# Latent cross attention on one core: layer norm folded into the weights and the exponent, keys projected from a transposed context with split f32r matmuls, batch end moved into the next round

## What is computed

```
def layernorm(x, g, b):
    mu = jnp.mean(x, axis=-1, keepdims=True)
    var = jnp.mean((x - mu) ** 2, axis=-1, keepdims=True)
    return (x - mu) * jax.lax.rsqrt(var + LN_EPS) * g + b
def rmsnorm(x, gamma):
    norm = jnp.sqrt(jnp.sum(x * x, axis=-1, keepdims=True)) * x.shape[-1] ** (-0.5)
    return x / jnp.maximum(norm, RMS_EPS) * gamma
xn = layernorm(x, ln_x_g, ln_x_b)          # x: context, (32, 1601, 192)
ln = layernorm(latents, ln_l_g, ln_l_b)    # (32, 64, 256)
q = ln @ Wq.T
kv = jnp.concatenate([xn @ Wkv.T, ln @ Wlkv.T], axis=1)
k, v = kv[..., :INNER], kv[..., INNER:]    # 4 heads of 64
attn = einsum('bhid,bhjd->bhij', rmsnorm(q, qn_g) * SCALE, rmsnorm(k, kn_g))
attn = softmax(where(full_mask, attn, -max))
out = einsum('bhij,bhjd->bhid', attn, v) @ Wo.T + bo
```

## Time and profile before

| | before |
|---|---|
| median of 3 runs | 4133.69 us (4133.42 to 4134.72) |
| the profiled execution | 4131.72 us |
| its span, first to last instruction | 4129.9 us |
| stage `xa_` | 166.9 to 1659.0 us of the span |
| mean granted TensorE clock | 0.873 of full speed |
| busy: TensorE, VectorE, ScalarE, GpSimd | 3298.8, 2627.2, 1901.4, 315.2 us |

### The profile page before, as it was taken

How to read it: one execution, slowest core, us unless ns; L and a number is a source line. 1 busy time by engine, 2 the same in 40 slices (tenths; PEclk the granted TensorE clock), 3 DMA queues, 4 the chain that set the end, 5 groups by cost and what they waited for, 6 DMA issues and landing times. The chain is left out here.

```text
span 4129.9 us, 98958 instructions
## 1 busy us (share of the span) xinstructions
PE 3298.8 (80%) x34538; PEld 2869.4 (69%) x34538; DVE 2627.2 (64%) x8299; ACT 1901.4 (46%) x3959; POOL 315.2 (8%) x323
## 2 busy tenths in 40 slices
PE   3489999999999999445437999999999999753664
PEld 3378888888888888333326888888888888633443
DVE  5477777777777775476666777777677777455000
ACT  1145555555555554123224666666566666422110
POOL 0200000000000000000012111111111111000101
PEclk7689998999999998677667999999999999965786
DMA  1111111111111110200011111111111111121322
GB/s 62 59 35 37 38 43 38 39 41 39 39 42 39 38 42 12 67 20 20 10 31 37 39 39 40 39 42 37 39 40 39 40 39 39 45 65 57 124 91 76
DMA packets 206334, 181.47 MB, mean 44 GB/s; under 512 B 65260, under 2 KB 199457, under 8 KB 205728
## 3 DMA queue, kind: packets, MB, share of 16 engines
q1 hardware_dynamic: 203808, 168.59, 14.2%
q0 software_dynamic: 2048, 6.68, 0.5%
HBM read 146.95 MB, written 28.39 MB: 42 GB/s over the span
## 5 line engine op out<-in xcount | busy, mean ns | idle before, releaser
L1768 DVE CUSTOM_DVE_ANT_0 xb_junk<-xb_ring,xb_mbias 128x372 bf16<-128x372 f32 (+2 forms) x1024 | 544.4, 572 | 175.7 <-PE xb_ring L1676 153.5
L1607 ACT ACTIVATE xb_P<-xb_sc 124x1024 f32<-124x1024 f32 (+1 forms) x416 | 426.0, 1026 | 377.0 <-PE xb_sc L1700 374.7
L704 PE MATMUL xa_ring<-xa_wf,xa_xT 96*124 96x256 f32 (+1 forms) x1664 | 399.8, 391 | 18.6 <-DVE xa_xT L818 15.3
L704 PEld LDWEIGHTS xa_ring<-xa_wf,xa_xT 96*124 96x124 f32 (+1 forms) x1664 | 313.9, 192 | 76.7 <-issue 23.7
L679 PE MATMUL xa_acc<-xa_xhat,xa_P 124*128 124x193 f32 x1664 | 314.1, 330 | 0.0
L1647 PE MATMUL xb_ring<-xb_xst,xb_whi 128*128 128x372 f32 (+2 forms) x768 | 262.2, 369 | 38.7 <-DVE xb_xst L1747 32.8
L1676 PE MATMUL xb_ring<-xb_khi,xb_qhi 64*128 64x372 f32 (+2 forms) x1024 | 266.1, 401 | 27.4 <-DVE xb_klo L1753 17.2
L1647 PE MATMUL xb_ring<-xb_whi,xb_xst 128*124 128x256 f32 (+1 forms) x1248 | 285.3, 291 | 2.4
L1700 PE MATMUL xb_sc<-xb_qhi,xb_khi 64*124 64x256 f32 (+1 forms) x1664 | 281.7, 372 | 0.0
L1753 DVE TENSOR_TENSOR xb_klo<-xb_ring,xb_khi 128x372 fp32r<-128x372 f32 (+2 forms) x256 | 138.6, 571 | 210.3 <-ACT xb_khi L1573 209.4
L679 PEld LDWEIGHTS xa_acc<-xa_xhat,xa_P 124*128 124x128 f32 x1664 | 267.2, 190 | 5.5 <-issue 5.5
(11 more groups left out here) (391 smaller groups left out, 7475.5 us busy)
## 6 DMA issues: line engine op xcount, KB each, us to landing
xa_raw<-in_ctx SPq DMA_DIRECT2D x64, 279.0 KB
ex_w<-in_W SPq DMA_DIRECT2D x16, 1024.0 KB
xa_raw<-in_ctx SPq DMA_DIRECT2D x32, 372.0 KB
xb_raw<-in_ctxT SPq DMA_DIRECT2D x64, 186.0 KB
xb_raw<-in_ctxT SPq DMA_DIRECT2D x32, 248.0 KB
xa_mask<-in_mask SPq DMA_DIRECT2D x32, 200.1 KB
xb_mask<-in_mask SPq DMA_DIRECT2D x32, 200.1 KB
xa_raw<-in_ctx SPq DMA_DIRECT2D x32, 186.0 KB
```

What stands on the lines that cost most here:

```text
L704: i = nc.tensor.matmul(bank[0:KEYS, 256 * (t % 2):256 * (t % 2) + 256], xT[0:H + h, c % 2, h, t * KEYS:(t + 1) * KEYS], wf[0:H + h, h, 0:256],
L1607: nc.scalar.activation(P[0:w, pbuf(c, p), :], sc[(c + p) % 2][0:w, :], ACT.Exp).then_inc(sem("exped"), 1)
L1768: v.tensor_tensor_reduce(out=junk[:, k, 0:w], in0=ring[f % 3][:, 0:w], in1=mbias[:, p, k0:k0 + w], scale=1.0, scalar=-3.0e38, op0=ALU.add, ...
```

## The change

The layer norm no longer produces xhat. The mean is folded into the weights: from each column of the gained weight matrix wf its mean over the 192 inputs is subtracted (with the matrix `even`). Keys are projected as x W + sigma b, which is the old key times sigma, and the RMS norm removes the factor. The values use raw x with a column sigma beside it, and P is divided by sigma in the exponent: the Exp has the bias nlr = -ln(var + eps)/2, one per key.

x comes already transposed from memory (input ctxT, which the stage `xb_` reads too). x and the weights are split in f32r parts, high and low, and the keys are the sum of five f32r matmuls for each tile. The parts that make x: ScalarE rounds 128 rows to xh (L712), GpSimd rounds the other 64 rows twice (L670, L671), VectorE subtracts to get the low parts (L952, L953). sigma is split too, on a tile `sig`, transposed by TensorE (step ST) and copied to rows of xhs by ScalarE (L707).

The new steps: Y (VectorE's statistics), YA (ScalarE: Ln, Exp, Copy, and nlr on GpSimd), YB (VectorE: low part of sigma), ST, X (splitting x), RS and R (the former R1 and R2), Q (GpSimd's preparation of a batch), PV (the weighing, now a step of its own). Y, YA, YB, ST, X and the first chunk of K run two batches ahead of B. F1 and F2 of a batch move into the next round, after the ring. M goes through the ring and is copied by one ScalarE instruction. The Exp is split in two of 256 columns. raw is three batches deep, STEADY is 12.

```
-        ROUNDS = [("T", 0), ("X1", 1), ("M", 0), ("K", 0), ("B", 0), ("X2", 1), ("X1", 2), ("R1", 0), ("T", 1),
-                  ("R2", 0), ("B", 1), ("K", 1), ("KT", 0), ("X2", 2), ("B", 2), ("X1", 3), ("R1", 1), ("A", 0),
-                  ("T", 2), ("R2", 1), ("B", 3), ("X2", 3), ("K", 2), ("KT", 1), ("X1n", 0), ("R1", 2), ("B", 4),
-                  ("A", 1), ("T", 3), ("R2", 2), ("B", 5), ("K", 3), ("X2n", 0), ("R1", 3), ("B", 6), ("KT", 2),
-                  ("PVend", 0), ("R2", 3), ("A", 2), ("KT", 3), ("F0", 0), ("F1", 0), ("A", 3), ("AL", 0),
-                  ("mred", 0), ("F2", 0)]
+        ROUNDS = [("Q", 0), ("K", 1), ("B", 0), ("R", 0), ("X", 3), ("RS", 1),
+                  ("B", 1), ("PV", 0), ("KT", 0), ("R", 1), ("K", 2), ("Yn", 0), ("RS", 2),
+                  ("B", 2), ("YAn", 0), ("PV", 1), ("A", 0), ("KT", 1), ("R", 2), ("YBn", 0), ("F1", 0),
+                  ("B", 3), ("PV", 2), ("A", 1), ("STn", 0), ("Xn", 0), ("K", 3), ("RS", 3), ("Yn", 1),
+                  ("B", 4), ("YAn", 1), ("PV", 3), ("KT", 2), ("R", 3), ("YBn", 1), ("F2", 0), ("Yn", 2),
+                  ("B", 5), ("YAn", 2), ("PV", 4), ("A", 2), ("STn", 1), ("Xn", 1), ("KT", 3), ("YBn", 2), ("Yn", 3),
+                  ("B", 6), ("YAn", 3), ("PV", 5), ("A", 3), ("AL", 0), ("STn", 2), ("Xn", 2), ("YBn", 3), ("mred", 0), ("STn", 3),
+                  ("Kn", 0), ("RSn", 0), ("PV", 6), ("M", 0), ("F0", 0)]
...
                 if kind == "K":
-                    pe.wait_ge(sem("xT0"), nth(n, 4, c))
-                    pe.wait_ge(sem("xT1"), nth(n, 4, c))
+                    pe.wait_ge(sem("xlo"), nth(n, 4, c))
+                    pe.wait_ge(sem("srow"), nth(n, 4, c))
...
+                            nc.tensor.matmul(o, xh[:, keys], wh[:], start=True, stop=False)
+                            nc.tensor.matmul(o, xh[:, keys], wl[:], start=False, stop=False)
+                            nc.tensor.matmul(o, xhl[:, keys], whh[:], start=False, stop=False)
+                            nc.tensor.matmul(o, xl[:, keys], wh[:], start=False, stop=False)
+                            i = nc.tensor.matmul(o, xhs[:, keys], wls[:], start=False, stop=True)
...
+                if kind == "ST":
+                    pe.wait_ge(sem("siglo"), nth(n, 4, c))
+                    bank = room((kind, c, 0), n)
+                    for t in range(nt):
+                        i = nc.tensor.transpose(bank[0:96, t * KEYS:(t + 1) * KEYS], sig[0:KEYS, t0 + t, :].bitcast(F32), ident[0:KEYS, 0:KEYS])
+                    i.then_inc(sem("st_ps"), 1)
...
+                if kind == "YB":
+                    dve.wait_ge(sem("sighi"), nth(n, 4, c))
+                    v.tensor_tensor(sig[0:KEYS, t0:t0 + nt, 65], raw[0:KEYS, t3, t0:t0 + nt, DC], sig[0:KEYS, t0:t0 + nt, 64].bitcast(F32),
+                                    ALU.subtract).then_inc(sem("siglo"), 1)
+                if kind == "X":
+                    dve.wait_ge(sem("xhi"), nth(n, 4, c))
+                    dve.wait_ge(sem("xhi2"), nth(n, 4, c))
+                    cols = slice(k0, k0 + W)
+                    v.tensor_tensor(xl[:, cols], xTr[:, 0, cols], xh[:, cols].bitcast(F32), ALU.subtract)
+                    v.tensor_tensor(xhl[64:128, cols], xTr[0:64, 1, cols], xhl[0:64, cols].bitcast(F32), ALU.subtract).then_inc(sem("xlo"), 1)
...
+                    nc.gpsimd.tensor_copy(xhl[0:64, k0:k0 + W], xTr[0:64, 1, k0:k0 + W])
+                    nc.gpsimd.tensor_copy(xhs[0:64, k0:k0 + W], xTr[0:64, 1, k0:k0 + W]).then_inc(sem("xhi2"), 1)
...
+                    nc.scalar.activation(P[0:KEYS, b_, 0:256], s_[0:KEYS, 0:256], ACT.Exp, bias=nlr[0:KEYS, t, 2 * c:2 * c + 1])
+                    if c < 6:
+                        i = nc.scalar.activation(P[0:KEYS, b_, 256:512], s_[0:KEYS, 256:512], ACT.Exp, bias=nlr[0:KEYS, t, 2 * c + 1:2 * c + 2])
```

More of the change, by code:

```diff
@@ L465, in schedule, with there, one @@
+        while len(FILLS) % len(ring):
+            FILLS.append(None)
+        PLACE = {f[0]: n for n, f in enumerate(FILLS) if f}
+        def there(n):
+            return not isinstance(n, int) or 0 <= n < NB
         def schedule(engine_step, loop_engine, chain=None, per_round=0):
-            def one(n, p, do_a, do_b, do_next):
+            def one(n, s):
                 for kind, c in ROUNDS:
                     if kind in OF_B:
[L470 to L480, removed]
+                        if there(n):
+                            engine_step(kind, c, n, s % 6)
+                    elif kind in OF_LAST:
+                        if there(n - 1):
+                            engine_step(kind, c, n - 1, (s + 5) % 6)
+                    elif kind in OF_NEXT:
+                        if there(n + 2):
+                            engine_step(OF_NEXT[kind], c, n + 2, (s + 2) % 6)
+                    elif there(n + 1):
+                        engine_step(kind, c, n + 1, (s + 1) % 6)
@@ L481, in schedule @@
+            for n in (-2, -1, 0):
+                one(n, n + 6)
+            turns = (NB - 5) // STEADY
+            with loop_engine.Fori(0, turns) as i:
                 if chain:
@@ L685, in step @@
-            def step(kind, c, n, p):
-                t0, nt = CHUNKS[c % 4]
-                W = nt * KEYS
-                if kind == "T":
-                    pe.wait_ge(sem("xhat"), nth(n, 4, c))
-                    for h in range(2):
-                        bank = room((kind, c, h), n)
-                        hi = H + h
-                        for t in range(nt):
-                            i = nc.tensor.transpose(bank[0:hi, t * KEYS:(t + 1) * KEYS],
-                                                    xhat[0:KEYS, p, t0 + t, H * h:H * h + hi], ident[0:KEYS, 0:KEYS])
-                        i.then_inc(sem("xT_ps"), 1)
+                r, k = n - FILLS[f][4], f - 4
@@ new lines, in room @@
+                while True:
+                    if k < 0:
+                        k, r = k + len(FILLS), r - 1
+                        if isinstance(r, int) and r < -2:
+                            break
+                    if FILLS[k] is not None:
+                        _, name, per, j, d = FILLS[k]
+                        if there(r + d):
+                            pe.wait_ge(sem(name), nth(r + d, per, j))
+                            break
+                    k -= 4
+                return ring[f % 4]
@@ L730, in step @@
                     pe.wait_ge(sem("negmax"), nth(n, 1, 0))
-                    if not (isinstance(n, int) and n == 0):
-                        pe.wait_ge(sem("accT"), n)
+                    bank = room((kind, c, 0), n)
                     for o in range(2):
-                        i = nc.tensor.matmul(sc[0][0:33, 128 * o:128 * o + 128], negmax[:, o, :], ident[:], start=True, stop=True)
+                        i = nc.tensor.transpose(bank[0:65, 128 * o:128 * o + 128], negmax[:, o, :], ident[:])
                     i.then_inc(sem("m_ps"), 1)
                 if kind == "B":
-                    s = sc[(c + 1) % 2]
+                    s_ = sc[(c + p) % 2]
                     if c == 0:
```

439 lines of the change are left out of this document (258 added, 181 removed).

## The result

The change makes the kernel slower: 4456.59 us (median of 4 runs, 4455.23 to 4458.94) against 4133.56 (4 runs, 4133.00 to 4134.72), a ratio of 1.078, 95% interval 1.0765 to 1.0797. The forecast was 3980, faster. The profiled execution after took 4456.78 us, its span is 4455.0, the mean clock 0.844.

The account below looks back on a forecast made before the run. TensorE was taken as the bound; the steady round falls from 44.5 to 39.5 us, and 150 + 7 + 9 - 14 = 152 us off 4131.7 gives 3980. Range 3865 to 4050 us.

Parts of the forecast that it names:

- the last round: Last round, with no next batch: 29.1 us becomes PV, B, F1 and F2 only, about 20, saving 9.
- the start: Before the first F0: memory clearing 8 us, weights' delay 14, shorter first round 8; net 14 later, bounds 5 and 30.
- a sign that the forecast is wrong: Forecast wrong if TensorE's largest wait isn't ST 3's, the clock reads near 1.00, or VectorE is busy over nine tenths.
- The step that failed: DMA term: context loaded twice, 40 GB/s become about 75, but loads are issued a round or more ahead, costing nothing.
- GpSimd's additions: Casts, second mask row and small operations add 6.8 us a round on GpSimd; contention with VectorE costs 0.3.
- the sum: Steady round: 44.5 - 3.6 - 1.4 - 0.2 - 2.2 - 0.4 + 2.0 + 0.5 + 0.3 = 39.5 us.
- VectorE's tight row: Behind K 0: 13 us of VectorE work before F1 can use A 0's bank; 0.5 us of waits a round.
- ST 3's wait for YB 3: End of a round: TensorE waits 2.0 us for VectorE, bounds 1.0 and 3.0, then half clock for about 6.8 us.
- the first rival: The wait comes but the clock holds, 3878 us, or ST 3 hardly waits, 3818 us; chance 0.26.
- K: Key projection on TensorE: 26 f32 matmuls, 11.26 us, become 65 in f32r, 7.64 us; gain 3.6 a round.
- F1's wait for latn: TensorE's wait before F1 goes because F1 comes a third of a round later; gain 2.2 us a round.
- The last rival: Slower than before: every added GpSimd operation holds VectorE for its own length, 6.8 us a round; 4175 us; chance 0.04.

Follow-up runs that it names:

- experiment 1: Changed kernel with step Q moved from the head of the round to behind X 3: 4231.9 us.
- experiment 5: Changed kernel with the small loads issued behind B 6's scores instead of behind PV 6, Q left at the head: 4167.0 us.
- experiment 2: Changed kernel with GpSimd's two casts of X writing 4 columns instead of 372 or 496 in the batch loop: 4444.3 us.
- experiment 11: kernel 8 with GpSimd's casts of X writing 4 columns instead of 372 or 496 in the batch loop: 4037.9 us.
- experiment 9: kernel 8 with the seven folded-weight loads issued behind the first three context loads: 4035.3 us, first F0 at 320.4.
- experiment 10: kernel 8 with batch 2's first context loads issued behind batch 1's transposed context: 4036.5 us, first F0 at 321.2.
- experiment 13: kernel 8 plus three ST steps later, weight loads early and batch 2's context behind batch 1's transposed context: 3975.1 us, 0.9617 of the kernel before.
- kernel 6: kernel 4 with F1 moved behind PV 2: 4052.8 us.
- kernel 8: kernel 4 with F1 moved behind PV 2 and the small loads issued behind B 6's scores: 4040.4 us.
- kernel 4: Changed kernel with Q moved behind X 3 and YB 3 ahead of X 2: 4118.1 us.

## Why the prediction was wrong

The difference to the forecast is 477 us of the span: 29 steady rounds at 54.75 in place of 39.5, 442; round 30, which was to be 7 us shorter, 36.5 in place of 32.5, 4; the last round as forecast; the start 29; the rest of the program 1.

Of the 15.3 us that a steady round is too long, TensorE is idle for 11.9 and busy for 3.4. The clock can account for the 3.4: it is at half for 17 us of a round in place of 6.8, which by estimate costs up to 5 us. That the largest wait of TensorE was another than ST 3's was named beforehand as a sign that the forecast is wrong.

- **The step that failed** is in the part on GpSimd and DMA: "The loads are issued a round or more ahead. Nothing." It holds for raw and xT. It doesn't for the four small loads, which SyncE issues behind PV 6 and for which Q waits at the head of the very next round, with X 3's casts behind it on GpSimd. I had GpSimd's additions as lengths (6.8 us, near enough: 8.5 in all, 9 forecast) and as contention (0.3), and never asked what each of them stands behind in its queue. Experiments 1 and 5, two different ways to take the wait away, give 225 and 290 us back.
- **What is left behind that step**: the kernel of experiment 5 is still 187 us above the forecast. Its steady round is 44.8 us, 5.3 too long, and its waits are 7.9 us a round where the sum had 2.8: ST 3.7, F1 for a bank 2.1, KT for khat 1.2 and for the maxima 0.9. The sum had one wait of ST and 0.5 for A 0's bank, and nothing for KT.
- **The evidence was at hand.** That GpSimd waits through each round for small loads could be read in the trace before; it cost nothing there, as nothing urgent stood behind. The change put the casts of X in the same queue, and those of X 3 directly behind it.
- **VectorE's tight row** behind K 0 was seen, with X 3 in it, and priced at 0.5 us of waits, on the ground that TensorE comes as late. That reckoned with VectorE's work only; with the row held for 7.5 us by another engine KT 1 stands still.
- **ST 3's wait for YB 3**: forecast 2.0, measured 2.7 on average. Right in mechanism and place, and within its bounds. The fall of the clock came with it in 21 of 29 rounds, mostly for 3.4 us in place of 6.8; in the other eight the clock held, as the first rival had it. The longest slow stretch came with the wait I hadn't seen, 10 to 14 us.
- **K**: starts 0.12 us apart, as in the earlier trace rows. TensorE's busy time fell by 1.9 us a round, though 17 us of the round ran at half clock. F1's wait for latn is gone; the one for A 0's bank, forecast at 0.5, is 1.9.
- **The last rival**, GpSimd's operations holding VectorE for their full length, had the right sign and the right pair of engines, at 4175, and the wrong mechanism. The Trainium skill, page "SBUF — State Buffer", section "Who interferes with whom", warns of such contention. Where the two meet the trace agrees. After, in the start of the stage, a subtraction without and one with GpSimd's mask row beside it:
```profile
228.65 0.55 DVE L952 TENSOR_TENSOR xa_xl<-xa_xTr,xa_xh 128x372 fp32r<-128x372 f32 x1 [1.88 <-ACT xa_xh L712]
...
233.03 1.72 DVE L952 TENSOR_TENSOR xa_xl<-xa_xTr,xa_xh 128x372 fp32r<-128x372 f32 x1 [1.88 <-ACT xa_xh L712]
```
```profile
232.82 1.53 POOL L648 TENSOR_SCALAR xa_mbias<-xa_mask 128x1612 bf16<-128x1612 uint8 x1
```
0.55 us became 1.72. But in the loop they hardly meet, and experiments 2 and 11 price the length of the casts, some 2.7 us a round, at 12 and 3 us.
- **The start** was forecast 14 us late, bounds 5 and 30, and was 43. Clearing memory held the first load by 9.7 us (182.50 against 172.78), 8 forecast. The weights' delay was named; the second delay, batch 2's context in SyncE's queue in front of batch 1's transposed context, was not, and by experiments 9, 10 and 13 it had to go too before either gave anything. With both gone the first F0 is at 298.3.
- **The range** failed with them: it took in bounds of the known terms and no case in which a moved step stands behind a wait on an engine that the sum called hidden.

## What to carry to other kernels

An engine that executes in order is hidden only as long as nothing that others need stands behind its longest wait: before work is given to an idle engine, read what that engine idles for and where in its order, not only for how long. When a step is added, follow it through each queue that it passes: what is ahead of it, which of those waits for a DMA, and when that DMA is issued. A delay that proves to be worth nothing when it alone is taken away may have a second one behind it, so take both away before it is dropped.

## What was new about the hardware

- The length of one wait didn't settle what the clock did. Before, it fell in every round, at F1's wait of 2.2 us or within some 2 us behind it. After, of 18 waits of ST 3 of 2.4 to 2.5 us it fell in ten and stayed at 1.00 in eight; at the 11 longer ones, up to 3.2 us, it fell each time. At KT 1's waits of some 7 us it fell each time, between 0.8 and 4.6 us into the wait. Waits that are nearly all between 0.4 and 2.0 us, several in a round, left it at 1.00 in 26 of 29 rounds of kernel 6 and in 15 of 29 of kernel 8. What decides it is open.
- GpSimd's mask row of 1612 columns is slowed by VectorE as well: 1.53 us in after, and here, in kernel 4, 2.32 us beside VectorE's multiplication for khat (up to 2.34 in its 32 executions there):
```profile
936.96 0.96 DVE L966 TENSOR_TENSOR xa_khat<-xa_ksb,xa_krn 124x768 f32<-124x768 f32 x1
```
```profile
936.99 2.32 POOL L648 TENSOR_SCALAR xa_mbias<-xa_mask 128x1612 bf16<-128x1612 uint8 x1 [13.88 <-DMA xa_vlat<-vl]
```
